# Preactivated attention convolution: the residual x is added by accumulating DMA transfers inside SBUF, issued by GpSimd, instead of by VectorE

## The reference, cut to what matters

```python
xn = gn(x)                                           # 32 groups
h = relu(bn(mean(xn) @ fc_w.T))
ch_att, fl_att = sigmoid(h @ ch_w.T + ch_b), sigmoid(h @ fl_w.T + fl_b)
kn_att = softmax(h @ kn_w.T + kn_b)
agg_w = einsum('bk,koc->boc', kn_att, weight)
y = einsum('bchw,boc->bohw', xn * ch_att, agg_w) * fl_att
return x + ((y - bn_m) * inv + bn_b)
```

## Time and profile before

| | |
|---|---|
| time, median of 2 runs | 2114.56 us (2114.48 to 2114.63) |
| span of the profiled execution | 2112.4 us |
| what lies around the span (median less span) | 2.2 us |
| TensorE busy | 97% |
| VectorE busy | 88% |
| ScalarE busy | 82% |
| GpSimd busy | 0% |
| mean DMA rate | 197 GB/s |

### The profile page before, as it was taken

One profiled execution on the slowest core, in us unless ns is written; L12 is line 12 of the kernel. 1 busy time (PEld: TensorE's weight loads), 2 busy tenths in 40 slices (PEclk: granted clock), 3 DMA queues, 4 the chain that ended last, 5 costly groups with the idle time before them and its releaser, 6 DMA issues.

```text
span 2112.4 us, 33140 instructions
## 1 busy us (share of the span) xinstructions
PE 2056.3 (97%) x10948; PEld 1078.1 (51%) x10948; DVE 1867.6 (88%) x2886; ACT 1729.7 (82%) x2295; POOL 0.2 (0%) x4
## 2 busy tenths in 40 slices
PE   1999999999999999999999999999999999999998
PEld 0455555555555555555555555555555555555554
DVE  7889889889889899889899898898898998898973
ACT  4788888888888888888888888888888888888885
POOL 0000000000000000000000000000000000000000
PEclk9999999999999999999999999999999999999999
DMA  8465556565556565556655565665565655566522
GB/s 332 139 209 194 204 189 206 200 208 203 195 193 208 195 206 202 196 191 208 208 200 200 191 208 193 208 208 191 191 208 202 206 200 192 195 205 207 175 105 105
DMA packets 237284, 415.99 MB, mean 197 GB/s; under 512 B 7248, under 2 KB 236624, under 8 KB 236752
## 3 DMA queue, kind: packets, MB, share of 16 engines
q1 hardware_dynamic: 237264, 415.74, 57.6%
HBM read 210.19 MB, written 205.52 MB: 197 GB/s over the span
## 4 chain that ended last, share of the span: by engine, by line
PE 97%; DVE 1%; DMA 1%; ACT 1%; SPq 0%; issue 0%; DVEq 0%
PE product L679 32%; PE product L680 32%; PE product L681 32%; DMA x_ring<-x 1%; DVE mixed_weight L529 0%; DVE chunk_stats L349 0%; PE small L649 0%; SPq L193 0%; DVE w_lo L545 0%; PE small L640 0%; ACT y L290 0%; PE small L644 0%; ACT x_norm L227 0%; DVE x_lo L357 0%; ACT x_hi L236 0%
## 5 line engine op out<-in xcount | busy, mean ns | idle before, releaser
L679 PE MATMUL product<-x_hi,w_hi 128*128 128x448 f16 x3584 | 1264.5, 353 | 6.7 <-DVE x_lo L357 3.7
L680 PE MATMUL product<-x_lo,w_hi 128*128 128x448 f16 x3584 | 1264.6, 353 | 0.0
L681 PE MATMUL product<-x_hi,w_lo 128*128 128x448 f16 x3584 | 1264.4, 353 | 0.0
L245 ACT ACTIVATE y<-product,out_bias,out_scale 128x448 f32<-128x448 f32 x896 | 641.8, 716 | 275.2 <-PE product L681 270.5
L227 ACT ACTIVATE x_norm<-x_ring,norm_bias,norm_scale 128x448 f32<-128x448 f32 x896 | 671.1, 750 | 1.3 <-DVE norm_bias L409 1.3
L363 DVE TENSOR_TENSOR x_ring<-x_ring,y 128x896 f32<-128x896 f32 x448 | 481.5, 1087 | 100.0 <-ACT y L245 95.7
L679 PEld LDWEIGHTS product<-x_hi,w_hi 128*128 128x128 f16 x3584 | 356.1, 99 | 327.3 <-issue 5.1
L681 PEld LDWEIGHTS product<-x_hi,w_lo 128*128 128x128 f16 x3584 | 350.9, 98 | 328.2 <-issue 1.6
L680 PEld LDWEIGHTS product<-x_lo,w_hi 128*128 128x128 f16 x3584 | 350.8, 98 | 319.5 <-issue 1.3
L349 DVE BATCH_NORM_STATS2 chunk_stats<-x_ring 128x6 f32<-128x448 f32 x896 | 493.4, 616 | 1.3 <-DMA x_ring<-x 1.2
L357 DVE TENSOR_TENSOR x_lo<-x_norm,x_hi 128x1792 f16<-128x1792 f32 x224 | 452.4, 2019 | 19.7 <-ACT x_hi L236 19.7
(11 more groups left out here) (66 smaller groups left out, 261.5 us busy)
## 6 DMA issues: line engine op xcount, KB each, us to landing
x_ring<-x SPq DMA_DIRECT2D x224, 896.0 KB, 4.8
out<-x_ring SPq DMA_DIRECT2D x224, 896.0 KB, 3.9
weight<-wt SPq DMA_DIRECT2D x4, 1024.0 KB, 15.1
params<-par SPq DMA_DIRECT2D x1, 462.0 KB, 3.4
```

What stands on the lines that cost most here:

```text
L245: nc.scalar.activation(y[:, s % 2, t], acc[k % BANKS][:, 0:COLS], ACT.Identity, bias=obias[:, t:t + 1], scale=oscale[:, u, t:t + 1]).then_ ...
L679: nc.tensor.matmul(bank, whi[:, u, t, cols], hi, start=(t == 0), stop=False)
L680: nc.tensor.matmul(bank, whi[:, u, t, cols], lo, start=False, stop=False)
L681: ins = nc.tensor.matmul(bank, wlo[:, u, t, cols], hi, start=False, stop=(t == CT - 1))
```

## The change

VectorE's `add` is gone. GpSimd gets a loop of its own: for every half of every chunk it waits for the evacuation, issues a DMA from `y` to `x_ring` that adds instead of overwriting, waits until that DMA has landed (`half_in`), and then raises `add_done`. The next half is issued only after that. ScalarE, TensorE and SP have the same instructions and waits as before; the semaphore `add_begun` has no reader. On VectorE the wait for the complete statistics moves from the start of step 2 to the end of step 1, where a copy of 4 columns stands behind it.

```diff
-            def add(turn, s, half):
-
-                dve.wait_ge(evac_done, turn.at(4 * RING, BANKS + 4 * s + 2 * half + 2))
-                two = slice(2 * half, 2 * half + 2)
-                nc.vector.tensor_tensor(xs[:, s, two], xs[:, s, two], y[:, s % 2, two], ALU.add).then_inc(add_done, 1)
...
                     for t in range(CT):
-                        if t == 0 and s:
-                            if prepare and n == 2:
-                                stats_complete(turn, b)
-                            add(turn, s - 1, 1)
+                        if prepare and (n, t) == (1, 3):
+                            for f, tile in stats_at(s, t):
+                                if not (last and f >= RING):
+                                    stats(turn, f, tile)
+                            stats_complete(turn, b)
+                            step(nc.vector.tensor_copy(tmp[:, :], bst[:, b % 2, :, 0, 0]))
+                            continue
...
-                        if t == 2:
-                            add(turn, s, 0)
...
+        @block.gpsimd
+        def _(pool):
+            def add(turn, s, half):
+
+
+                pool.wait_ge(evac_done, turn.at(4 * RING, BANKS + 4 * s + 2 * half + 2))
+                pool.sem_inc(add_begun, 1)
+                two = slice(2 * half, 2 * half + 2)
+                pool.dma_start(xs[:, s, two], y[:, s % 2, two], accum_op=ALU.add).then_inc(half_in, 16)
+                pool.wait_ge(half_in, turn.at(32 * RING, 16 * (2 * s + half + 1)))
+                pool.sem_inc(add_done, 1)
+
+            pool.sem_inc(add_done, 4)
+
+            def body(i):
+                turn = Turn(pool, i)
+                for s in range(RING):
+                    for half in range(2):
+                        add(turn, s, half)
```

More of the change, by code:

```diff
@@ L165, in build @@
         add_done = sem("add_done")
+        half_in = sem("half_in")
+        add_begun = sem("add_begun")
         ln_ready = sem("ln_ready")
@@ L342, in after @@
                 dve.wait_ge(order, turn.at(2 * STEPS, done[0]))
-            STEPS = 24 + CT
+            STEPS = 25 + CT
             def stats(turn, f, t):
@@ L485, in _ @@
             start = Turn(dve, 0)
-            dve.sem_inc(add_done, 4)
             nc.vector.memset(ones[:, :], 1.0).then_inc(const_ready, 1)
@@ L629, in body @@
                         assert done[0] - before == STEPS, done[0] - before
-                add(turn, RING - 1, 1)
             with dve.Fori(0, TURNS - 1) as i:
@@ L633, in _ @@
             body(TURNS - 1, True)
+        @block.gpsimd
[13 more added lines that the diff above has]
+                        add(turn, s, half)
+            with pool.Fori(0, TURNS - 1) as i:
+                body(i)
+            body(TURNS - 1)
         @block.tensor
```

## The result

The changed kernel takes **2703.03 us** (median; 2702.38 to 2703.69) against 2114.56: a ratio of 1.279, 95% interval 1.275 to 1.282. It is 588 us slower. The forecast was 2935 us, slower, with a range of 2110 to 3605 us.

What follows compares the result with a forecast made beforehand. TensorE bounds the kernel now; after the change GpSimd's serial transfers would. 61.2 us before the first add, 448 × 6.4 = 2867 us, 4.3 us tail and 2.2 us span-to-median give 2935 us; range 2110 to 3605 us.

Steps and rivals of the forecast that it cites:

- The bound and the worth of the removal: In the loop only TensorE sets the pace, 4.57 us a half; removing 481.5 us of VectorE adds is worth nothing.
- start, tail and launch terms: Outside the 448 halves: 61.2 us before the first add, 4.3 us after the last store's issue, 2.2 us span to median.
- L: Time of one half, from its transfer's issue to landing plus GpSimd's turn to the next: 6.4 us, against TensorE's 4.57.
- landing alone: Adding transfer of one half without SP's traffic, both operands read, priced by the load's row: 4.8 us.
- of it the bytes, both operands counted: Reading y and x_ring for one half, 2 × 448 KB, at the fastest stretch's 350 GB/s: 2.62 us.
- of it the fixed part: What a transfer's landing takes beside its bytes: 2.2 us by the load's row, 1.3 by the store's.
- collisions, mean: Delay of a half's add by SP's stores and loads on the shared DMA engines: 1.2 us, between 0.5 and 2.7.
- GpSimd's own turn: GpSimd writing descriptors, raising add_done and waiting, for each half: 0.4 us beyond the load's row, an estimate.
- The loads: SP's loads come later by the same rhythm; VectorE's statistics wait for them inside the slack that ScalarE's wait opens.
- Hidden: Rival: a half's transfer and turn stay at or below 4.57 us, behind TensorE; 2117 us, chance 0.17.
- DMA engines as the bound: Rival: adds and SP's traffic fill the DMA engines nearly without gaps, 10.6 us a chunk; 2440 us, chance 0.12.
- Slow accumulation: Rival: adding or descriptor writing costs several us more, 8 to 9.5 us a half; 3876 us at 8.5, chance 0.16.

Runs made afterwards that it cites:

- thin traffic: Changed kernel with SP's loop stores and loads cut to 64 KB instead of 896 KB, adding transfers kept: 2324.84 us, ratio 1.099.
- the copy: Changed kernel with its 448 GpSimd transfers copying y over x_ring instead of adding it: 2344.60 us, ratio 1.109.

## Why the prediction was right, and where its terms were off

**The bound and the worth of the removal: right.** TensorE set the pace, and the run without any add shows 2113.56 us.

**The mechanism: right.** GpSimd's chain paces the kernel, every half passes through whole, and the start, tail and launch terms of 68 us held within 2 us (the tail is 6.0 us, not 4.3, by GpSimd's DRAIN). The forecast was 232 us too high, all of it in L: 6.4 us foretold, 5.88 found, 448 × 0.52 = 233 us. By term:

| term of L | foretold, us | measured, us | from |
|---|---|---|---|
| landing alone | 4.8 | 4.2 | least landing, also the median with thin traffic |
| of it the bytes, both operands counted | 2.62 | 2.58 of the engines' time | 0.428 × 2700.6 / 448 |
| of it the fixed part | 2.2 | 1.6 | 4.2 - 2.6 |
| collisions, mean | 1.2 | 0.9 | half of 6.03 - 4.21 |
| GpSimd's own turn | 0.4 | 0.7 | 1015.41 to 1016.13, of it 0.50 ahead of the issue |

The mis-sized term is the fixed part. I took it from the load's row (2.2 us of 4.8) where the store's (1.3 us of 3.9) was nearer. The measured 1.6 us hold an issue of 0.86 us, against 0.39 for SP's; why it is shorter than a load's is not shown. The other two errors cancel, and that is luck: the collisions were taken 0.3 us too high, and the turn of GpSimd, for which I had no row, 0.3 us too low. That a store starts just when the next add is issued did not speak for the upper part of 0.5 to 2.7 us: it does so for every second add only, and the 0.9 us are 1.8 us and nothing in turn.

**The Trainium skill's fit** (DMA: Bandwidth & Descriptors, Anatomy of one DMA — SWDGE (gpsimd) path), 3.05 us for these bytes, is near what the copy shows undisturbed (2.7 us). It does not hold for the adding transfer, 4.2 us. The rule that a reducing transfer reads twice (Collectives: The Full Stack, The bandwidth ceiling: the fold count and why AG ≠ RS ≠ AR) agrees with the trace in size: 2.58 us of the engines for an add, 0.215 × 2339.7 / 448 = 1.12 us for a copy, a ratio of 2.3. The page says it of the reduce step of a collective, and the read itself is not seen here. Both together, 4.1 us, came within 0.1 us of the undisturbed landing, and yet by them the change would be hidden: they lack GpSimd's turn and the collisions, 1.6 us, which decide here. That 4.1 comes so near is in part luck too: its fixed part of 2.0 us is 0.4 more than the 1.6 measured, and its bytes, 2.1 us, are 0.5 less than the 2.58.

**The loads: right for the time, wrong for TensorE.** I said that statistics would wait for loads inside the slack, that TensorE would idle 1.8 us in each half, and that the clock would cost nothing. The waits of the changed kernel (us in total, times, longest):

```profile
DVE chunk_stats L351 <- DMA x_ring<-x: 858.5, 154, 9.9
...
ACT y L247 <- POOLq L640: 510.7, 214, 9.3
ACT y L247 <- PE product L699: 352.1, 167, 8.8
```

ScalarE's wait before L247 was foretold near 800 us. It is 865.6 us, but only 510.7 of them are behind an add; 352.1 are behind TensorE. VectorE waited 858.5 us for loads. In the kernel before, the same group (its last column) had waited 1.2:

```profile
L349 DVE BATCH_NORM_STATS2 chunk_stats<-x_ring 128x6 f32<-128x448 f32 x896 | 493.4, 616 | 1.3 <-DMA x_ring<-x 1.2
```

The idle time of TensorE came in stalls of up to 9.7 us, not in even small ones. Some stand behind ScalarE's evacuations (155.3 us), more behind `x_lo` and the means (140.5 and 145.2 us, 24.6 of the latter at the start), which stand in VectorE's queue behind statistics that wait for a load. One of them, step by step:

```profile
1048.22 2.21 DVE L351 BATCH_NORM_STATS2 chunk_stats<-x_ring 128x6 f32<-128x448 f32 x4 [9.41 <-DMA x_ring<-x]
1050.34 2.01 DVE L359 TENSOR_TENSOR x_lo<-x_norm,x_hi 128x1792 f16<-128x1792 f32 x1
1052.48 0.55 PE L697 MATMUL product<-x_hi,w_hi 128*128 128x448 f16 x1 [8.50 <-DVE x_lo L359]
```

And the clock fell. Its stretches in the loop (us, TensorE busy (xinstructions), clock, DMA share, GB/s):

```profile
1048.00:1056.00 8.00, 3.52 (x12) 0.57 0.83 210
1056.00:1060.00 4.00, 2.61 (x14) 1.00 0.97 281
1060.00:1064.00 4.00, 0.57 (x3) 0.78 0.61 144
1064.00:1070.00 6.00, 6.00 (x21) 0.58 1.02 270
```

After idle stretches it worked at the lower of its two levels (1.2 GHz; clock 1.00 in the rows is 2.4 GHz), so its busy time rose from 2056.3 to 2198.3 us and its share is 81%, not the 70% foretold (2056.3 us would be 76% of this shorter span). It is 3% of the chain that ended last, so this cost little that the chain shows: in its faster stretches TensorE caught up with the adds again.

**The rivals.** Hidden: it needed L at or below 4.57 us, and the undisturbed 4.93 was too much already, 0.36 us over. DMA engines as the bound, foretold at 2440 us: not the limit of the changed kernel, but the next one behind it, and 2452 us when it was made to decide. Slow accumulation at 8 to 9.5 us: excluded, since the undisturbed landing is 4.2 us, 1.5 us above the copy's, and 0.3 of that is the issue.

## What to carry to other kernels

Work that is moved off an engine which is not the bound gains nothing, and its new place must keep the bound's rhythm. Before an add is given to a DMA, hold the time of one round (the transfer's landing, the issuing engine's turn, and a collision with what lands beside it) against that rhythm, and the engines' time, with the bytes counted twice (an add took 2.3 times a copy's here), against the share that is free. With transfers that wait for each other, half as many of them can be free where all of them cost 28%.

## What the runs showed that had not been expected

- Shorter transfers collided more: with the copy the added wait for a half was about 1.7 us (median landing 4.4, least 2.7), with the add 0.9 us. SP's store and load are tied to the same `add_done`, so they move closer as the rhythm shortens.
- GpSimd's issue is 0.86 us for an accumulating transfer at 1792, 3584 and 7168 bytes a row alike (386.5, 385.4 and, for 224, 193.3 us), and 0.54 us for a copying one.
- TensorE's clock was at its lower level in parts of the loop, its busy time grew by 142 us, and it is still only 3% of the chain that ended last.
- A program whose GpSimd issues transfers closes with a DRAIN of 5.7 to 9.0 us on GpSimd, and in these runs the span ended with it.
